# Another order of the prologue, scores in one float32 product, and identity transposes in TensorE's waits

## What is computed

```python
def xattn(v, k, q, mask, W_merge, b_merge):          # called with ctx, ctx, layernorm(x)
    scores = jnp.einsum('bqd,bkd->bqk', q, k) * (1.0 / jnp.sqrt(d_k))
    att_map = jax.nn.softmax(jnp.where(mask, NEG_INF, scores), axis=-1)
    atted = jnp.swapaxes(jnp.einsum('bqk,bkd->bqd', att_map, v), -1, -2)
    return jnp.einsum('bdl,ol->bdo', atted, W_merge) + b_merge

rw = gating(h, sim_matrix, gates)                    # 16 weights for each row
q = jnp.einsum('bte,bted->btd', rw, jnp.einsum('btc,ecd->bted', h, q_proj))   # k and v likewise
scores = jnp.where(causal, jnp.einsum('bqd,bkd->bqk', q, k) * scale, -jnp.inf)
attn = jnp.einsum('bqk,bkd->bqd', jax.nn.softmax(scores, axis=-1), v)
out = jnp.einsum('bted,edc->btc', attn[:, :, None, :] * rw[..., None], o_proj)
```

## Time and profile before

| | |
|---|---|
| median of three runs | 906.52 us |
| the profiled execution, its own time | 906.4 us |
| span in its trace | 904.7 us (1.7 us lie around it) |
| busy: TensorE, VectorE, ScalarE, GpSimd | 873.0, 642.6, 226.3, 129.1 us |
| first matmul of slot 0 starts at | 37.44 us |
| first wait of VectorE for a slot's matmuls (from which it is no longer behind) | 65.58 us |
| mean granted clock of TensorE | 0.992 |

### The profile page before, as it was taken

The page is one execution under the profiler, slowest core; times in us unless marked ns, Lnnn a source line. Parts: engine busy times, 40 slices in busy tenths (PEclk is TensorE's granted clock), DMA queues, the critical chain, the costliest instruction groups (busy, mean ns, idle before and its releaser), DMA issues.

```text
span 904.7 us, 15909 instructions
## 1 busy us (share of the span) xinstructions
PE 873.0 (96%) x4872; PEld 815.1 (90%) x4872; DVE 642.6 (71%) x1964; ACT 226.3 (25%) x570; POOL 129.1 (14%) x335
## 2 busy tenths in 40 slices
PE   4689999999999999999999999999999999999998
PEld 4579999989999899998999999999999989999996
DVE  6888877766677675867767677776767767575674
ACT  4522322213122131212212132121312212121121
POOL 3321111201111110111101111120111201011100
PEclk9799999999999999999999999999999999999999
DMA  9825513254151541415314262244514143040302
GB/s 298 301 81 175 164 58 94 75 128 150 39 148 33 143 136 50 130 38 163 103 60 118 61 174 81 75 106 98 179 38 126 55 123 103 25 107 26 106 25 93
DMA packets 68197, 96.99 MB, mean 107 GB/s; under 512 B 10905, under 2 KB 34105, under 8 KB 67874
## 3 DMA queue, kind: packets, MB, share of 16 engines
q1 hardware_dynamic: 67554, 95.18, 35.7%
q10 hardware_dynamic: 576, 1.05, 0.3%
HBM read 77.07 MB, written 19.14 MB: 106 GB/s over the span
## 4 chain that ended last, share of the span: by engine, by line
issue 65%; PE 19%; POOLq 9%; POOL 3%; DMA 2%; DVE 1%; DVEq 0%; ACT 0%; SPq 0%
PE psQ L1302 11%; PE psM L1403 2%; POOLq L615 2%; PE psO L1403 2%; POOLq L595 2%; POOLq L618 2%; PE psQ L1403 1%; POOL limit L598 1%; POOLq L612 1%; POOLq L597 1%; POOLq L620 1%; DMA XT<-in_x_t 1%; POOL pow_out L621 1%; POOL pow_tmp L611 1%; DMA merge_lo<-merge_scratch 1%
## 5 line engine op out<-in xcount | busy, mean ns | idle before, releaser
L1302 PE MATMUL psQ<-Wqkv_hi,hT_hi 128*128 128x384 f32 (+1 forms) x1024 | 352.0, 344 | 1.6 <-DVE hT_lo L878 1.4
L1302 PE MATMUL psQ<-Wqkv_lo,hT_hi 128*128 128x384 f32 (+1 forms) x1024 | 347.7, 340 | 0.0
L1302 PE MATMUL psQ<-Wqkv_hi,hT_lo 128*128 128x384 f32 (+1 forms) x1024 | 347.5, 339 | 0.0
L1012 DVE SCALAR_TENSOR_TENSOR acc<-psQ,RW,acc 128x192 f32<-128x192 f32 x448 | 164.6, 411 | 119.0 <-PE psQ L1302 117.0
L1302 PEld LDWEIGHTS psQ<-Wqkv_hi,hT_hi 128*128 128x128 f32 x1024 | 193.8, 189 | 8.1 <-DVE hT_lo L878 1.8
L1302 PEld LDWEIGHTS psQ<-Wqkv_lo,hT_hi 128*128 128x128 f32 x1024 | 194.2, 190 | 4.6
L1302 PEld LDWEIGHTS psQ<-Wqkv_hi,hT_lo 128*128 128x128 f32 x1024 | 193.6, 189 | 0.0
L610 POOL TENSOR_TENSOR pow_tmp<-b_mv,eps 128x1 f32<-128x1 f32 x32 | 8.3, 258 | 673.6 <-DVE b_mv L965 673.6
L834 ACT ACTIVATE mixedT_hi<-spread 128x512 fp32r<-128x512 f32 x64 | 40.5, 632 | 190.1 <-DVE spread L1191 146.3
L1403 PE MATMUL psO<-Wo_hi,mixedT_hi 128*128 128x512 f32 x120 | 51.6, 430 | 0.2 <-DVE mixedT_lo L1179 0.2
L1179 DVE TENSOR_TENSOR mixedT_lo<-spread,mixedT_hi 128x512 fp32r<-128x512 f32 x64 | 43.6, 681 | 5.7 <-ACT mixedT_hi L834 4.8
(11 more groups left out here) (205 smaller groups left out, 1309.6 us busy)
## 6 DMA issues: line engine op xcount, KB each, us to landing
spread<-gates_scratch SPq DMA_DIRECT2D x30, 512.0 KB, 6.7
X<-in_x SPq DMA_DIRECT2D x32, 256.0 KB, 2.7
x_scratch<-X SPq DMA_DIRECT2D x32, 256.0 KB, 2.0
resid<-x_scratch SPq DMA_DIRECT2D x32, 256.0 KB, 4.3
out<-resid SPq DMA_DIRECT2D x32, 256.0 KB, 2.1
merge_hi<-merge_scratch SPq DMA_DIRECT2D x28, 256.0 KB, 3.0
merge_lo<-merge_scratch SPq DMA_DIRECT2D x28, 256.0 KB, 3.7
XT<-in_x_t SPq DMA_DIRECT2D x27, 256.0 KB, 2.9
```

The costliest lines, as they stand in the source:

```text
L1012: dve.scalar_tensor_tensor(out=acc[e][:], in0=src, scalar=w, in1=acc[e][:], op0=ALU.mult, op1=ALU.add).then_inc(expert_added, 1)
L1302: last = pe.matmul(psQ[g % 4][:, 0:first_col(g) + PW], a[:, c * P:(c + 1) * P], w[:, c, E + g * PW - first_col(g):E + (g + 1) * PW], start ...
```

## The change

- The scores of tiles 0 to 4 are one float32 product, `x1_whole_score`: the turned rows as loaded, and a float32 copy of the context (`ctx_f`), 4 products of 77 columns. The high and low parts of the turned rows (`turned_high`, `turned_low`), and for batch 0 those of the context, go away; `x1_limit` reads the bank in its scaling instruction instead of after a copy and an addition. ScalarE makes the float32 copies (`copy_whole_ctx`, and `whole=` in `copy_ctx` for batch 1, whose parts are still made).
- `keep_busy(turns)`: so many float32 transposes of the identity into `psQ[3]`, at eight places of TensorE's prologue: 16 ahead of the context, 6 ahead of the first score and after each of the four, 8 ahead of `sum_x2`, 20 after it, 8 after `move_rows`.
- The order: context 1 is loaded right after the gates, centred between `merge_high(3)` and `x1_exp(3)`, and transposed between the third and fourth quarter of `sum_G`. The `sim` sums come after score 1, their power on GpSimd ahead of the limits of tile 3. Turned tile 1 is loaded ahead of the first centring. `w_high(0)` comes after `G_high`, `w_low(0, 0)` after `row_stats`, `w_low(1)` and the sigmoid after `low_rows`. Pair 1's weights are loaded after the bias rows. ScalarE runs six pairs ahead (`W_AHEAD`) where it ran four.

```diff
+W_AHEAD = 6
+BUSY = {"ctx": 16, "score": 6, "G": 8, "stats": 20, "rows": 8}
...
+        ctx_f = [spread[:, 4 + 2 * n:6 + 2 * n, :].rearrange("p a l -> p (a l)")[:, 0:KC * CP].rearrange(
+            "p (c k) -> p c k", c=KC) for n in range(2)]
...
                 for n in range(TILES):
                     sp.dma_start(merge_raw[:, n, :], merge_t[:, n * D:(n + 1) * D]).then_inc(ld_merge[n], 16)
                 sp.dma_start(gate_e, gates.partition_broadcast(P)).then_inc(ld_gates, 16)
+                sp.dma_start(ctx_first[1], ctx_in[1]).then_inc(ld_ctx[1], 16)
...
                 sp.dma_start(MASK[:, TILES, :], row(mask, TILES)).then_inc(ld_x[TILES], 16)
-                sp.dma_start(ctx_first[1], ctx_in[1]).then_inc(ld_ctx[1], 16)
-                load_w(1)
                 sp.wait_ge(bias_made, 2)
                 sp.dma_start(G[0][C:CP, :].bitcast(F32), bias_hi.bitcast(F32)).then_inc(bias_placed, 16)
                 sp.dma_start(G[1][C:CP, :].bitcast(F32), bias_lo.bitcast(F32)).then_inc(bias_placed, 16)
-                for g in range(2, PAIRS):
+                for g in range(1, PAIRS):
                     load_w(g)
                 keep_x2(0)
...
-                pool.wait_ge(sim_floored, 1)
-                pool.tensor_tensor(sim_rn, sim_ss, half_e, ALU.pow).then_inc(sim_rooted, 1)
+                    if n == 2:
+                        pool.wait_ge(sim_floored, 1)
+                        pool.tensor_tensor(sim_rn, sim_ss, half_e, ALU.pow).then_inc(sim_rooted, 1)
...
+                def copy_whole_ctx():
+                    for c in (0, 2):
+                        act.wait_ge(moved, moves.step())
+                        act.activation(ctx_f[0][:, c:c + 2, 0:C], ctx_bank(psT[moves.bank()]), ACT.Copy
+                                       ).then_inc(moved_lo, 1)
+
+                def copy_ctx(chunks=(0, 2), whole=None):
                     for c in chunks:
                         act.wait_ge(moved, moves.step())
+                        if whole is not None:
+                            act.activation(whole[:, c:c + 2, 0:C], ctx_bank(psT[moves.bank()]), ACT.Copy
+                                           ).then_inc(whole_ctx, 1)
                         act.activation(ctxT[:, c:c + 2, 0, 0:C], ctx_bank(psT[moves.bank()]), ACT.Copy
...
-                act.dma_start(xt_first[0], turned(0)).then_inc(ld_xt[0], 16)
+                for n in range(2):
+                    act.dma_start(xt_first[n], turned(n)).then_inc(ld_xt[n], 16)
                 act.wait_ge(ld_ctx[0], 16)
                 centre(ctx_first[0], centre_dump, 0)
-                for n in range(1, TILES):
+                for n in range(2, TILES):
                     act.dma_start(xt_first[n], turned(n)).then_inc(ld_xt[n], 16)
-                act.wait_ge(dve_init, 1)
-                copy_ctx()
-                turned_high(0, 0)
-                turned_high(1, 1)
+                copy_whole_ctx()
                 act.wait_ge(ld_bias, 16)
                 act.activation(bias_hi, bias_f, ACT.Copy).then_inc(bias_made, 1)
                 moves.step()
                 x1_exp(0, 0)
-                turned_high(2, 0)
                 x1_high(0, 0, 0, 0)
                 merge_high(0)
                 moves.step()
                 x1_exp(1, 1)
-                turned_high(3, 1)
                 x1_high(1, 1, 1, 0)
                 merge_high(1)
                 act.wait_ge(ld_gates, 16)
@@ -749,32 +752,33 @@
                 merge_high(2)
                 x1_high(2, 2, 0, 0)
                 merge_high(3)
-                w_high(0)
+                act.wait_ge(ld_ctx[1], 16)
+                centre(ctx_first[1], centre_dump, 1)
                 moves.step()
                 x1_exp(3, 1)
                 x1_high(3, 3, 1, 0)
+                act.wait_ge(dve_init, 1)
+                copy_ctx(whole=ctx_f[1])
                 slice_high(0)
-                turned_high(TILES, 0)
                 G_high(0)
+                w_high(0)
                 act.wait_ge(sim_normed, 1)
                 act.activation(simn[0], sim_f, ACT.Copy).then_inc(sim_hi, 1)
+                moves.step()
                 w_high(1)
-                act.wait_ge(ld_ctx[1], 16)
-                centre(ctx_first[1], centre_dump, 1)
-                moves.step()
-                copy_ctx()
                 w_high(2)
                 copy_rows(0)
                 slice_high(1)
-                w_high(3)
+                for g in range(3, W_AHEAD):
+                    w_high(g)
 
                 def body(b, qkv, lead):
                     for k in range(SLOTS):
                         j, g, prepare, cross, attn, ab = job_lists(k, b, qkv, lead)
                         t = TILES * b + j
                         t1, p1, q1 = t + X1_LEAD, (j + 1) % 2, (j + 1) % TILES
-                        if qkv and is_first(b) and k + 4 < PAIRS:
-                            w_high(k + 4)
+                        if qkv and is_first(b) and k + W_AHEAD < PAIRS:
+                            w_high(k + W_AHEAD)
                         if qkv and is_first(b) and k == SCORE_4_SLOT:
                             moves.step()
                         if qkv and is_first(b) and k == PAIRS:
...
                     bank = psT[moves.bank()]
-                    dve.tensor_copy(sc[p][:], bank[:, CP:CP + C])
-                    dve.drain()
-                    dve.tensor_tensor(sc[p][:], bank[:, 0:C], sc[p][:], ALU.add).then_inc(moved_lo, 1)
-                    dve.drain()
-                    dve.wait_ge(x1_scale_ready, t1 + 1)
-                    dve.wait_ge(limit_ready, t1 + 1)
-                    dve.scalar_tensor_tensor(out=sc[p][:], in0=sc[p][:], scalar=x1_scale[p][:, 0:1],
-                                             in1=limit[p][:], op0=ALU.mult, op1=ALU.min)
+                    if isinstance(t1, int) and t1 < X1_LEAD:
+                        dve.wait_ge(x1_scale_ready, t1 + 1)
+                        dve.wait_ge(limit_ready, t1 + 1)
+                        dve.scalar_tensor_tensor(out=sc[p][:], in0=bank[:, 0:C], scalar=x1_scale[p][:, 0:1],
+                                                 in1=limit[p][:], op0=ALU.mult, op1=ALU.min).then_inc(moved_lo, 1)
+                    else:
+                        dve.tensor_copy(sc[p][:], bank[:, CP:CP + C])
+                        dve.drain()
+                        dve.tensor_tensor(sc[p][:], bank[:, 0:C], sc[p][:], ALU.add).then_inc(moved_lo, 1)
+                        dve.drain()
+                        dve.wait_ge(x1_scale_ready, t1 + 1)
+                        dve.wait_ge(limit_ready, t1 + 1)
+                        dve.scalar_tensor_tensor(out=sc[p][:], in0=sc[p][:], scalar=x1_scale[p][:, 0:1],
+                                                 in1=limit[p][:], op0=ALU.mult, op1=ALU.min)
                     dve.drain()
                     dve.tensor_reduce(x1_max[p][:], sc[p][:], AX.X, ALU.max, negate=True).then_inc(x1_max_ready, 1)
...
                 dve.wait_ge(pool_init, 5)
                 dve.wait_ge(ld_x[0], 16)
                 x1_moments(0, 0, x_first[0])
-                low_ctx()
-                turned_low(0, 0)
+                moves.step()
+                moves.step()
                 dve.wait_ge(ld_x[1], 16)
                 x1_moments(1, 1, x_first[1])
-                turned_low(1, 1)
                 x1_limit(0, 0)
                 dve.wait_ge(ld_x[2], 16)
                 x1_moments(2, 0, x_first[2])
                 x1_invert(0, 0)
-                turned_low(2, 0)
                 x1_low(0, 0, 0)
                 x1_limit(1, 1)
+                dve.wait_ge(sim_summed, 1)
+                dve.tensor_scalar(sim_ss, psM[:, 0:E], NORM_FLOOR ** 2, None, ALU.max).then_inc(sim_floored, 1)
                 dve.wait_ge(ld_x[3], 16)
                 x1_moments(3, 1, x_first[3])
                 x1_invert(1, 1)
-                turned_low(3, 1)
                 x1_low(1, 1, 1)
                 x1_limit(2, 0)
                 merge_low(0)
@@ -1044,36 +1050,32 @@
                 merge_low(1)
                 x1_low(2, 2, 0)
                 x1_limit(3, 1)
-                dve.wait_ge(sim_summed, 1)
-                dve.tensor_scalar(sim_ss, psM[:, 0:E], NORM_FLOOR ** 2, None, ALU.max).then_inc(sim_floored, 1)
                 merge_low(2)
                 x1_invert(3, 1)
                 merge_low(3)
                 x1_low(3, 3, 1)
-                slice_low(0)
-                dve.wait_ge(ld_x[TILES], 32)
-                x1_moments(TILES, 0, x_first[TILES])
-                turned_low(TILES, 0)
                 dve.wait_ge(sim_rooted, 1)
                 for c in range(KC):
                     last = dve.tensor_tensor(sim_f[:, c, :], sim_f[:, c, :], sim_rn, ALU.mult)
                 last.then_inc(sim_normed, 1)
+                low_ctx()
+                slice_low(0)
+                dve.wait_ge(ld_x[TILES], 32)
+                x1_moments(TILES, 0, x_first[TILES])
+                G_low(0)
```

(58 more changed lines are left out.)

27 lines of the change are left out of this document (9 added, 18 removed).

## The result

| | before | after |
|---|---|---|
| median (lowest to highest), us | 906.81 (905.36 to 909.47), 10 runs | 902.46 (900.4 to 905.49), 10 runs |
| profiled execution, us | 906.4 | 902.1 |
| ratio after to before | | 0.9946, 95% interval 0.9932 to 0.9961 |

A forecast was written before the change was run, and what follows sets the result against it. TensorE bounds the kernel after 65.58 us, VectorE's chain and backlog before it. `low_rows` 5.1 us earlier plus 0.2 at the backlog make 5.3 off 906.4: 901.1, as median 901.2 us; range 899.0 to 905.8.

The forecast's parts named there:

- What bounds the kernel: After 65.58 us TensorE is busy 819.3 of 824.4 us, untouched by the change; what can be won lies ahead.
- Start of scoring: Prologue up to the first score: context transposes at 5.75, sixteen turns 3.4 us and hidden, first score ready at 9.3.
- The rounds: Four scoring rounds on VectorE: 2.5 us each instead of 3.2, with a new wait for the `sim` sums after limit 1.
- The load that was to hold `x1_exp(2)`: ScalarE in scoring: gates' load lands at 15.9, the sigmoid's exponential stands ahead, so `x1_exp(2)` starts at 16.2, not 15.2.
- Just in time: Scoring on GpSimd: limits of tile 3, queued behind a power, end at 17.8, for VectorE's limit 3 at 17.85.
- From `add_x2` to `low_rows`: Statistics, powers, normalising and transposes: 6.3 us less 0.2 for transposes at full clock; `low_rows` 5.1 us earlier.
- The backlog: VectorE's work behind `low_rows`: 0.85 and 0.65 more, 1.35 and up to 0.7 back; net 0.2 us gained.
- the first rival: Turns do not raise TensorE's clock, which then bounds scoring: only 0.7 and 0.5 us earlier, 905.3 us; chance 0.24.
- The second: Rival: turns in TensorE's queue cost too much, 0.345 us each, making the kernel 9.4 us later, 915.8 us; chance 0.07.
- The third: Rival: context 1's or the gates' load needs 11 us or more, `x1_exp` moves 1 to 3 us, 903.2 us; chance 0.12.

The follow-up runs named there:

- slice_late: After with the context's second slice moved behind weights 3 to 5 on ScalarE and behind `w_low(3)` on VectorE; 902.25 us, 0.9945 of before.
- power_back: After with GpSimd's power of the `sim` sums moved from ahead of the last limits back to behind them; 902.03 us, 0.9941 of before.
- no_turns: After with all 82 turns taken out, order and float32 scores kept; 901.53 us, 0.9939 of before.
- turns_slots: After with 24 more turns ahead of slot 4 and 36 ahead of slot 6's transposes, in batch 0; 902.71 us, 0.9941 of before.
- turns_slot6: After with 24 more turns ahead of slot 6's transposes only, in batch 0; 901.59 us, 0.9940 of before.
- moments_after_G: After with the fifth tile's moments put behind `G_low` instead of ahead of it; 900.64 us, 0.9936 of before.
- before_turns: Before with the 82 turns alone, in its old order; 907.43 us, 1.0004 of before.

## Why the prediction was right, and where by luck

**What bounds the kernel** held: after 62.99 TensorE is busy 99.3% (821.36 of 827.01), and what was won lies ahead. **Start of scoring** held within 0.2: context at 5.51 (5.75 said), sixteen turns 3.68 and later six 0.82, that is, less the last one's own 0.476 and 0.27, 0.21 and 0.11 for one (0.21, 0.12), score 1.83 and 1.01 (1.9, 0.9), first scaling 9.23 (9.3). The clock rose later than the start of scoring here; in slice_late it was up at 5.79. The rounds took 2.43 and 2.96 us (2.5 said, the second with the `sim` wait), and limit 2 is at its place (15.2).

**The load that was to hold `x1_exp(2)`** didn't. I had put the gates' landing at 15.9, issue time 7.04 plus 8.9. In after it is issued at 6.39, since the four merge loads ahead of it took 1.85 us to issue instead of 2.51, and ScalarE's exponential at 14.79 waits for nothing:

```profile
...
14.79 0.20 ACT L749 ACTIVATE spread<-spread 128x16 f32<-128x16 f32 x1
15.27 0.36 ACT L706 ACTIVATE sc<-sc,x_max 128x77 f32<-128x77 f32 x1 [0.28 <-DVE x_max L925]
...
```

`x1_exp(2)` is at 15.27 (16.2 said). The 0.9 won there brought nothing at the next step: the fourth scaling is at 17.82, about where I had it (17.85), but held by GpSimd, 0.99 of wait, not by ScalarE. "Just in time" was a coincidence of two late chains, and the one I had called hidden was the bound: power_back shows it, 16.22 without the power ahead. `x1_exp(3)` came right behind the centring and the fourth maximum (18.48; 19.6 said), so `sum_G` ended at 20.98 (21.95), `G_low`, for VectorE's queue alone as said, at 22.69 (23.5), and `add_x2` 1.75 behind at 24.44 (25.5).

**From `add_x2` to `low_rows`** I took 0.2 off 6.3; it is 5.53, 0.76 less. The transposes of `H` at 2.4 GHz give 0.49 of it (1.12 to 0.63), as the gap was filled with turns; no_turns has them at 1.09 and `low_rows` 0.56 later. I had bounded this by 0.45 and taken half. Another 0.14 came as the transposes no longer wait for the context's copy, which released them in the earlier trace rows. The last 0.13 lies ahead of `H`, where GpSimd's addition ahead of its powers took 0.81 us (L613) instead of 0.95 (L610 of before). So `low_rows` came 6.7 earlier, not 5.1: 1.1 of the difference is `add_x2`, which was 6.0 earlier instead of 4.9, and 0.6 is this step.

**The backlog** was to give +0.2 net. Slot 7 is 6.12 earlier, 0.6 less than `low_rows`, so the step is wrong by 0.8. Its terms stand, 0.85 and 0.65 lost, 1.35 and 0.7 at score 4 won, +0.55 together. Two waits were missed: the 0.71 at 35.62, for the slice's load, and 0.31 at 55.48, where VectorE, through with score 4 sooner, waits 0.47 instead of 0.16 for GpSimd's limit (L601). I had noted that the DMA engines are full and used it to say that pair 7 lands no later, but not that a small load issued at 26.55 behind the weights would land at 33.9 and hold ScalarE's high parts, and through them VectorE. With `low_rows` at 31.6 this would have cost less; each us won ahead of it is lost there. slice_late shows its price, 0.9. VectorE did not wait for slots again until 60.72 (60.3 said), which is near by luck: in no_turns, with slots 7 and 8 at full clock, it is 59.51. Slots 4 to 7 didn't wait for weights.

**The clock behind the wait** ahead of slot 7 was not in the sum at all. I had read 0.50 from 32.0 to 37.4 and that slots 0 to 3 ran low, at no price, since VectorE is later there; the same clock on slots 7 and 8, where VectorE has caught up, costs 1.5 in this trace. That the turns moved it there is not shown: turns_slots, whose instructions are those of after up to slot 4, had the half clock from 12.6 to 15.5 and from 29.2 to 32.6, where after's trace has none, so the place of such a stretch is not fixed by the instructions alone.

So the sum of 5.3 was met (4.3 to 4.4, interval 3.5 to 6.2) by three errors that largely cancel: +1.6 at `low_rows`, -0.8 at the backlog, -1.5 at slots 7 and 8. They leave 4.6, the lead at slot 9. The order of the steps was right, the nearness of the number is luck. One reading of the forecast's own was off: its range up to 905.8 does not leave out "a good part" of the first rival (904.3 to 906) but takes in most of it. **The first rival**, turns that don't raise the clock, falls: the clock rose while TensorE had done nothing but identity turns and four small transposes. TensorE of slice_late, which says it most plainly:

```profile
...
1.42 3.68 PE L1277 MATMUL psQ<-ident 128*128 128x128 f32 x16 [1.42 <-POOL eps L592]
5.44 0.51 PE L1235 MATMUL psT<-ident,spare_wo 77*128 77x77 f32 x4 [0.34 <-ACT spare_wo L677]
5.79 0.82 PE L1277 MATMUL psQ<-ident 128*128 128x128 f32 x6
...
12.41 1.49 PE L1277 MATMUL psQ<-ident 128*128 128x128 f32 x6
...
```

The last row shows that turns raise the clock but do not keep it: here it fell again at about 12, behind a wait of 0.81 us at 10.55, and was back at 15.3. The Trainium skill ("TensorE: Matmul & The Clock Gate", Part 4: PE-mode transpose) says that the full clock does not engage for transposes. For these float32 turns the traces disagree: six of them in 0.82 us, where at 1.2 GHz six take 1.49. The rival's own time, with turns at low clock, no run could show; but scores and sums at 1.2 GHz, without turns, cost 0.56 at slot 0 and nothing at slot 4, so of what the forecast gave the clock hardly anything reached the end. **The second**, turns that cost too much, holds nowhere in after, but its mechanism is real: turns_slots shows 2.3 us for a series longer than the wait that it fills. **The third**, a late load, happened with another load than the two named.

## What to carry to other kernels

When the work ahead of a floor is shortened, look for the next wait of each engine in the chain (here ScalarE, for a small load queued behind large ones) and repair the waits together: three edits, each worth 0.9 to 1.4 us at some landmark, gave nothing that could be told from after when made alone, and 2.7 us in the median together. Two of them, once combined, turned out to win the same time. Keeping a clock up is worth only what the waiting engine behind it can use: compare with the filler removed before keeping it, and never make it longer than the wait.

## What the runs showed of the hardware

- Identity turns of float32, 0.21 us each at 1.2 GHz and 0.11 at 2.4, raise the clock within the prologue, but not at a set time and not to stay: with the same instructions ahead, six turns first took 0.82 us at 5.79 in slice_late, at 8.17 in turns_slot6 and at 10.98 in after; in slice_late, moments_after_G and turns_slots the clock was low again from about 12.5 to 15.4.
- The half clock on slots 7 and 8 stood behind a wait of 3.1 us in both traces that have it, and behind one of 3.43 in before_turns it did not come.
- Clock and view can disagree: in the first microseconds of after, and in before up to 27.7 us, the view prints 1.00 where spacings are those of 1.2 GHz. I went by the spacing.
- A load of one slice (38.5 KB), issued behind the weights' loads, took 7.3 us from issue to landing in after, and 8.2 and 8.0 in power_back and moments_after_G.
- A GpSimd instruction stops VectorE even for an instruction of two columns, 0.23 us to 3.37. It shows in small in power_back, where VectorE's 0.30 us subtraction took 1.33 beside one of 1.26 on GpSimd that touches one partition (L644).
